# New order tables for the attention stage of a two-layer token kernel

## The chip, the cores and the metric

The kernel runs on one core of one Trainium2 chip. The metric is the device time of one execution in microseconds (us). The engines are TensorE (PE in the profile, PEld for its weight loads), VectorE (DVE), ScalarE (ACT), GpSimd (POOL) and SyncE (SP); each works its own list of instructions in order and waits for the others by semaphores. Three runs of the kernel before took 1610.21, 1616.7 and 1690.98 us.

## The reference, cut to what matters

Sixteen items of 256 tokens, 256 features each, go through two layers. Layer 0 pools an item by masked softmax weights and feeds it to 32 experts. Layer 1 multiplies an item by a matrix that its token picks, and runs a transformer block: attention, then 8 experts. The change lies in layer 1's attention (the cut is mine; 8 batches of 512 in the reference's shape names are 16 items of 256 here):

```python
x = x + L0_ffn(L0_cond(x))                 # 32 experts, top 4
h0 = x @ W[cat_id] + b[cat_id]             # one matrix per item
h = layernorm(h0, ln1_g, ln1_b)
q, k, v = split(h @ Wqkv)                  # 16 heads of 16
q, k = rope(q), rope(k)
scores = where(causal, q @ k.T / sqrt(16), -1e9)
attn = (softmax(scores) @ v) @ Wproj
h1 = h0 + attn
gates = softmax(layernorm(h1, ln2_g, ln2_b) @ Wgate)   # top 2 of 8 experts
x = x + h1 + moe(...)
```

## The kernel before, in words

Four stages follow each other: the pooling, layer 0's experts, the attention stage, and layer 1's experts. In the attention stage an item b is worked in steps, each a few instructions:

- **In front.** POOL gathers the item's rows of layer 0's results with 8 indirect DMAs (`got`, line 1293); DVE adds them, weighted (`combine`, line 1562); PE turns the item (`x_turn`), multiplies it by its matrix (`matrix`, line 1323), DVE normalises (`norm`, `scale`), with POOL working out the inverse deviation (line 1274), and PE turns the result back (`norm_turn`), which ACT copies to hT1.
- **Queries and keys.** For each half of the tokens PE makes queries and keys (`qk`, line 1413), DVE multiplies them by cosines and sines (line 1594), POOL adds and subtracts the products (lines 1302, 1303). PE turns the queries (`turn_qk` 0) and the keys (`turn_qk` 1). The `split` of each takes the high part on ACT (line 1492) and the low part on DVE (line 1598). Then SP's `stack` (line 1269) copies these parts with 8 DMAs of 128 KB for the queries into QS and 8 for the keys into KS. QS and KS are double buffers over items; the parts' tile `parts_qk` is single, as is `rm`, the tile of the rotated products.
- **Attention.** There are 4 groups of heads, and 3 parts of scores in each. PE makes `scores` (lines 1338 to 1347), DVE takes the negated row maximum (`row_max`, line 1554), ACT the exponentials (`exp`, line 1460), PE turns them (`turn_p`, line 1366), ACT copies them (line 1468), PE multiplies by the values (`values`, lines 1379 and 1381) and ACT copies the outcome (line 1474). `v` makes the item's values.
- **Behind.** `outputs` (line 1427) turns the results back and divides them by their sums, `out_turn`, `proj` (line 1323 again), the residual (`base` on POOL, line 1306), the second `norm` and `scale`, `gate_turn` and `gate`. Once for two items the routing follows (`route_shift`, `route_exp`, `route`, `rank`, `place`), and POOL scatters its table with 8 indirect DMAs (`entry`, line 1315).

What sets the order is written out by hand: PE_ROUND, DVE_ROUND, ACT_ROUND, POOL_ROUND and SP_ROUND, one table for each engine. An entry is a step, an offset and further indices. The function `rounds` goes over i from -4 on, and in round i it emits each entry for item i + offset, if there is such an item. So ("scores", -1, 3, 0) in round i is part 0 of group 3 of item i - 1. The engines don't meet at the ends of rounds: a round of one engine may begin well before that of another.

The waits that matter here: the first scores of an item wait until all 16 stack DMAs of that item have landed (line 1333), `stack` 0 waits until the scores of the item two before are done (line 1263), a split waits until the stack of the item before has landed (line 1491), `combine` waits for 4 gathers, and each light step of PE (all but scores, turn_p and values) uses one of two banks in turn and waits until what stood there two light steps before has been copied out (lines 1200 to 1203).

Of the kernel before, what the change touches and what calls it, by code (L numbers as in the profile page):

```python
# [91 lines left out]
def bass_adaln_ffn(nc, io, out):  # L92
    ctx = ExitStack()
    with ctx:
        return _build(nc, ctx, io, out)


def _build(nc, ctx, io, out):
# [6 lines left out]
    def sb(name, shape, dt=F32, scope=ctx):  # L105
        return scope.enter_context(nc.sbuf_tensor(name, shape, dt))
# [5 lines left out]
    normed = nc.dram_tensor("normed", (N + 1, D), F32, kind="Internal").ap()  # L112
# [10 lines left out]
    place = ExitStack()  # L123
# [204 lines left out]
    gate = sb("gate", [P, 2, 512], scope=layer0)  # L328
# [717 lines left out]
    def dve_experts0(e):  # L1046
# [89 lines left out]


    PE_ROUND = (
        ("scores", -1, 0, 1), ("x_turn", 1), ("scores", -1, 0, 2), ("qk", 0, 0), ("scores", -1, 1, 0),
        ("qk", 0, 1), ("scores", -1, 1, 1), ("gate_turn", -3), ("values", -2, 3), ("turn_p", -1, 0, 2),  # L1140
        ("turn_p", -1, 0, 0), ("gate", -3), ("outputs", -2, 0), ("turn_p", -1, 0, 1), ("scores", -1, 1, 2),
        ("turn_qk", 0, 0), ("scores", -1, 2, 0), ("scores", -1, 2, 1), ("outputs", -2, 1), ("turn_p", -1, 1, 2),
        ("values", -1, 0), ("scores", -1, 2, 2), ("out_turn", -2), ("turn_qk", 0, 1), ("turn_p", -1, 1, 0),
        ("turn_p", -1, 1, 1), ("scores", -1, 3, 0), ("proj", -2), ("scores", -1, 3, 1), ("matrix", 1),
        ("turn_p", -1, 2, 2), ("values", -1, 1), ("turn_p", -1, 2, 0), ("scores", -1, 3, 2),
        ("turn_p", -1, 2, 1), ("rank", -3), ("v", 0), ("turn_p", -1, 3, 2), ("values", -1, 2), ("norm_turn", 1),
        ("turn_p", -1, 3, 0), ("turn_p", -1, 3, 1), ("scores", 0, 0, 0))
    DVE_ROUND = (
        ("row_max", -1, 1, 2), ("split", 0, 0), ("outputs", -2, 1), ("row_max", -1, 2, 0), ("route", -3, 1),
        ("row_max", -1, 2, 1), ("row_max", -1, 2, 2), ("route", -3, 2), ("split", 0, 1), ("route", -3, 3),  # L1150
        ("row_max", -1, 3, 0), ("proj", -2), ("row_max", -1, 3, 1), ("matrix", 1), ("norm", 1, 0),
        ("norm", -2, 1), ("row_max", -1, 3, 2), ("scale", 1, 0), ("place", -3), ("combine", 2, 1),
        ("row_max", 0, 0, 0), ("row_max", 0, 0, 1), ("scale", -2, 1), ("row_max", 0, 0, 2), ("qk", 1, 0),
        ("row_max", 0, 1, 0), ("qk", 1, 1), ("row_max", 0, 1, 1), ("combine", 3, 0), ("gate", -2),
        ("route_shift", -2), ("outputs", -1, 0))
    ACT_ROUND = (
        ("exp", -1, 2, 2), ("exp", -1, 3, 0), ("turn_p", -1, 2, 2), ("exp", -1, 3, 1), ("values", -1, 1),
        ("turn_p", -1, 2, 0), ("turn_p", -1, 2, 1), ("exp", -1, 3, 2), ("turn_p", -1, 3, 2), ("v", 0),
        ("norm_turn", 1), ("values", -1, 2), ("turn_p", -1, 3, 0), ("exp", 0, 0, 0), ("x_turn", 2),
        ("exp", 0, 0, 1), ("turn_p", -1, 3, 1), ("exp", 0, 0, 2), ("gate_turn", -2), ("exp", 0, 1, 0),  # L1160
        ("values", -1, 3), ("turn_p", 0, 0, 2), ("exp", 0, 1, 1), ("turn_p", 0, 0, 0), ("turn_p", 0, 0, 1),
        ("split", 1, 0), ("exp", 0, 1, 2), ("route_exp", -2), ("turn_p", 0, 1, 2), ("exp", 0, 2, 0),
        ("out_turn", -1), ("split", 1, 1), ("turn_p", 0, 1, 0), ("exp", 0, 2, 1), ("values", 0, 0),
        ("turn_p", 0, 1, 1))
    POOL_ROUND = (
        ("got", 2, 1, 3), ("norm", 1, 0), ("got", 3, 0, 0), ("norm", -2, 1), ("got", 3, 0, 1), ("entry", -3, 0),
        ("got", 3, 0, 2), ("got", 3, 0, 3), ("qk", 1, 0), ("qk", 1, 1), ("entry", -3, 1), ("entry", -3, 2),
        ("got", 3, 1, 0), ("entry", -3, 3), ("got", 3, 1, 1), ("got", 3, 1, 2), ("base", -1))
    SP_ROUND = (
        ("normed", -2), ("weights", 3), ("stack", 1, 0), ("stack", 1, 1), ("base", -3))  # L1170
    ROUTING = ("route_shift", "route_exp", "route", "rank", "place", "entry")

    def rounds(table):
# [742 lines left out]
```

## Time and profile before

| | us |
|---|---|
| median of 3 runs | 1616.7 |
| the profiled execution, its own time | 1612.6 |
| span of the profile | 1610.8 |
| first scores of item 0 to first scores of item 15 | 494.1 |
| PE busy in those 494.1 us | 421.5 |

The profile is of one execution, told in microseconds from the start of its first instruction. "Idle before" is the time in which an engine stood still ahead of an instruction, with the one that released it behind the arrow; "issue" means that the profile shows no instruction that released it. A busy PE is matrix multiplications in its pipeline, not its peak. The granted clock is 1.00 at 2.4 GHz and 0.50 at 1.2 GHz. A share of DMA over 1 is packets in flight counted on top of each other.

### The profile page before, as it was taken

What the parts mean: (1) busy time and instruction counts of PE and PEld (TensorE: products, weight loads), DVE (VectorE), ACT (ScalarE), POOL (GpSimd) and SP (SyncE); (2) the same over time, 40 slices, a digit from 0 to 9 for tenths busy, and PEclk for the clock granted to TensorE, in tenths of its full rate; (3) what the DMA queues carried; (4) which work ended last, traced back from release to release, by engine and by line L of the source; (5) the groups of instructions that cost most, each with busy time, mean ns of one, the idle gap of its engine ahead of it and who ended that gap; (6) DMA issues with size and microseconds to landing.
All of it is one profiled execution on the core that took longest, in us unless ns stands there. A gap on an engine that the chain in (4) does not pass through costs nothing.

```text
span 1610.8 us, 27526 instructions
## 1 busy us (share of the span) xinstructions
PE 1414.7 (88%) x9776; PEld 1234.1 (77%) x9776; DVE 1026.3 (64%) x2435; ACT 905.2 (56%) x2156; POOL 720.0 (45%) x720
## 2 busy tenths in 40 slices
PE   7987699999999995679998898879826999999996
PEld 5776599999999984456776676656625999999996
DVE  3998477777777756456776776666524655555552
ACT  5886255555555531556776676757724554554452
POOL 0788644434343044333464554633243544554443
PEclk9989899999999997788999998999967999999999
DMA  6421365766666243765677666674543332433212
GB/s 182 138 60 29 87 190 163 191 173 183 181 178 189 78 131 61 109 108 112 125 123 139 122 116 124 116 126 73 73 142 96 93 67 62 97 95 87 50 22 27
DMA packets 139448, 182.00 MB, mean 113 GB/s; under 512 B 22485, under 2 KB 107296, under 8 KB 139312
## 3 DMA queue, kind: packets, MB, share of 16 engines
q1 hardware_dynamic: 111152, 128.28, 32.7%
q0 software_dynamic: 28160, 51.96, 16.2%
q8 instruction: 79, 1.29, 0.4%
q14 instruction: 57, 0.47, 0.1%
HBM read 107.28 MB, written 42.08 MB: 93 GB/s over the span
## 4 chain that ended last, share of the span: by engine, by line
PE 79%; issue 7%; DVE 5%; POOL 3%; DMA 2%; ACT 2%; SPq 1%; POOLq 0%; DVEq 0%; ACTq 0%
PE banks L921 47%; PE banks L1323 5%; PE banks L1366 5%; PE banks L1413 4%; PE banks L440 3%; PE banks L983 2%; PE banks L1379 2%; PE banks L1340 2%; PE banks L1338 1%; PE banks L597 1%; PE banks L1343 1%; PE banks L1347 1%; POOL table L1315 1%; PE banks L1760 1%; PE banks L1427 1%
## 5 line engine op out<-in xcount | busy, mean ns | idle before, releaser
L921 PE MATMUL banks<-hi_x,hi_w 128*128 128x320 f32 (+1 forms) x832 | 286.6, 344 | 10.8 <-DVE hidden L956 5.2
L921 PE MATMUL banks<-lo_x,hi_w 128*128 128x320 f32 (+1 forms) x832 | 285.3, 343 | 0.0
L921 PE MATMUL banks<-hi_x,lo_w 128*128 128x320 f32 (+1 forms) x832 | 285.0, 343 | 0.0
L921 PE MATMUL banks<-hi_w,hi_h 128*128 128x256 f32 x896 | 260.2, 290 | 2.1 <-DVE X L1010 1.7
L921 PE MATMUL banks<-lo_w,hi_h 128*128 128x256 f32 x896 | 253.5, 283 | 0.0
L921 PE MATMUL banks<-hi_w,lo_h 128*128 128x256 f32 x896 | 253.5, 283 | 0.0
L863 POOL DMA_INDIRECT xe<-pooled,idx x160 | 155.3, 971 | 199.9 <-PE banks L983 150.5
L1460 ACT ACTIVATE PN<-banks,smax 128x256 f32<-128x256 f32 (+1 forms) x512 | 181.8, 452 | 107.9 <-DVE smax L1554 107.0
L1747 POOL DMA_INDIRECT out<-X,tab x64 | 106.5, 1664 | 205.0 <-DVE X L1844 190.4
L921 PEld LDWEIGHTS banks<-hi_x,hi_w 128*128 128x128 f32 x832 | 158.0, 190 | 24.2 <-issue 10.6
L921 PEld LDWEIGHTS banks<-hi_w,hi_h 128*128 128x128 f32 x896 | 171.1, 191 | 3.3 <-issue 1.3
L921 PEld LDWEIGHTS banks<-lo_w,hi_h 128*128 128x128 f32 x896 | 171.4, 191 | 0.3
L921 PEld LDWEIGHTS banks<-hi_w,lo_h 128*128 128x128 f32 x896 | 171.2, 191 | 0.0
L1554 DVE TENSOR_REDUCE smax<-banks 128x2 f32<-128x512 f32 (+1 forms) x192 | 128.3, 683 | 63.1 <-PE banks L1340 56.9
L921 PEld LDWEIGHTS banks<-hi_x,lo_w 128*128 128x128 f32 x832 | 157.8, 190 | 13.2
L921 PEld LDWEIGHTS banks<-lo_x,hi_w 128*128 128x128 f32 x832 | 158.1, 190 | 11.8
L1293 POOL DMA_INDIRECT got<-done,slot x128 | 125.5, 981 | 88.9 <-DMA done<-res 56.8
L1805 ACT ACTIVATE hidden<-banks,b1s 128x512 f32<-128x512 f32 x128 | 87.9, 687 | 122.9 <-PE banks L921 122.9
L1833 DVE TENSOR_TENSOR lo_h<-hidden,hi_h 128x512 fp32r<-128x512 f32 x128 | 88.3, 691 | 76.5 <-ACT hi_h L1810 76.5
L956 DVE TENSOR_TENSOR hidden<-gate,banks 128x320 f32<-128x320 f32 (+1 forms) x144 | 73.4, 510 | 84.3 <-PE banks L921 75.0
L1468 ACT ACTIVATE PT<-banks 128x512 f32<-128x512 f32 x192 | 116.5, 624 | 15.1 <-PE banks L1366 14.8
L947 ACT ACTIVATE gate<-banks 128x320 f32<-128x320 f32 (+1 forms) x144 | 65.6, 456 | 98.1 <-PE banks L921 98.0
(186 smaller groups left out, 3082.6 us busy)
## 6 DMA issues: line engine op xcount, KB each, us to landing
w<-in_L_ffn_w SPq DMA_DIRECT2D x96, 256.0 KB, 5.9
done<-res SPq DMA_DIRECT2D x32, 640.0 KB, 3.9
QS<-parts_qk SPq DMA_DIRECT2D x128, 128.0 KB
KS<-parts_qk SPq DMA_DIRECT2D x128, 128.0 KB
BIG<-in_L_ffn_W SPq DMA_DIRECT2D x16, 1024.0 KB, 9.8
mask<-in_c_masks SPq DMA_DIRECT2D x16, 257.0 KB, 2.8
pooled<-XF SPq DMA_DIRECT2D x16, 256.0 KB, 3.2
WS<-in_L_cond_W SPq DMA_DIRECT2D x16, 256.0 KB, 2.7
```

The lines of the kernel that those rows point to most:

```text
L863: e.indirect_dma_start(xe[:, n % NXE, i, :], None, pooled, bass.IndirectOffsetOnAxis(ap=idx0[:, n * NS0 + i:n * NS0 + i + 1], axis=0)).the ...
L921: last = e.matmul(o, a[i], b[j], start=start and k == 0, stop=stop and k == 2, skip_group_check=True)
L956: e.tensor_tensor(hidden[:, i, 0:w], gate[:, i, 0:w], PS[:, up_bank(pt, unit) + 1, 0:w], ALU.mult).then_inc(s_hidden, 1)
L1293: e.indirect_dma_start(got0[:, b % NGA, t, k, :], None, done0, bass.IndirectOffsetOnAxis(ap=slot0[:, TB * b + t, k:k + 1], axis=0)).then_i ...
L1323: last = e.matmul(PS[:, bank, t * D:(t + 1) * D], src[:, c, t * P:(t + 1) * P], w(c), start=(c == 0), stop=(c == DC - 1))
L1366: last = e.transpose(PS[:, bank, k * P:(k + 1) * P], src, ident[:, :])
L1460: e.activation(PN[:, slot, part, x * width:(x + 1) * width], PS[:, part, x * width:(x + 1) * width], ACT.Exp, bias=smax[:, slot, col + x:c ...
L1468: e.activation(PT[:, G % NPN, part, :], PS[:, TBANK + n % 2, :], ACT.Copy).then_inc(s_pt, 1)
L1554: e.tensor_reduce(smax[:, G % NPN, col:col + heads_], PS[:, part, :].rearrange("p (x k) -> p x k", x=heads_), AX.X, ALU.max, negate=True). ...
L1747: e.indirect_dma_start(out_rows, bass.IndirectOffsetOnAxis(ap=who(u, i), axis=0), res1[:, u % 3, i, :], None, bounds_check=N - 1, oob_is_e ...
L1805: e.activation(hidden1[:, m % NHF, :], PS[:, 2 + m % 3, :], ACT.Gelu, bias=b1s[:, n, d:d + 1]).then_inc(s_hidden1, 1)
L1833: e.tensor_tensor(lo_h1[:, d, :], hidden1[:, m % NHF, :], hi_h1[:, d, :].bitcast(F32), ALU.subtract).then_inc(s_h1_lo, 1)
```

## The change

Only the five order tables are different. The steps themselves, what they wait for and what they compute are as before; tiles and buffers are too. In the old tables `qk`, `turn_qk` and `v` of item i stand in round i of PE, in places 4, 6, 16, 24 and 37 of 43, and the first scores of that item stand last in the same round. In the new ones those steps of item i + 1 stand in places 11, 12, 21, 23 and 29 of round i, and the first scores of item i in place 18. Around this `x_turn`, `matrix`, `norm_turn` move up in the same sense, and `values` (3), `outputs`, `out_turn` and `proj` of an item come one round earlier by their offset. On SP the order was normed, weights, the stacks, base, and becomes base, weights, the stacks, normed.

```diff
--- before.py
+++ after.py
@@ -1136,38 +1136,37 @@
 
 
     PE_ROUND = (
-        ("scores", -1, 0, 1), ("x_turn", 1), ("scores", -1, 0, 2), ("qk", 0, 0), ("scores", -1, 1, 0),
-        ("qk", 0, 1), ("scores", -1, 1, 1), ("gate_turn", -3), ("values", -2, 3), ("turn_p", -1, 0, 2),
-        ("turn_p", -1, 0, 0), ("gate", -3), ("outputs", -2, 0), ("turn_p", -1, 0, 1), ("scores", -1, 1, 2),
-        ("turn_qk", 0, 0), ("scores", -1, 2, 0), ("scores", -1, 2, 1), ("outputs", -2, 1), ("turn_p", -1, 1, 2),
-        ("values", -1, 0), ("scores", -1, 2, 2), ("out_turn", -2), ("turn_qk", 0, 1), ("turn_p", -1, 1, 0),
-        ("turn_p", -1, 1, 1), ("scores", -1, 3, 0), ("proj", -2), ("scores", -1, 3, 1), ("matrix", 1),
-        ("turn_p", -1, 2, 2), ("values", -1, 1), ("turn_p", -1, 2, 0), ("scores", -1, 3, 2),
-        ("turn_p", -1, 2, 1), ("rank", -3), ("v", 0), ("turn_p", -1, 3, 2), ("values", -1, 2), ("norm_turn", 1),
-        ("turn_p", -1, 3, 0), ("turn_p", -1, 3, 1), ("scores", 0, 0, 0))
+        ("rank", -3), ("scores", -1, 3, 0), ("turn_p", -1, 2, 2), ("scores", -1, 3, 1), ("values", -1, 1),
+        ("norm_turn", 1), ("turn_p", -1, 2, 0), ("turn_p", -1, 2, 1), ("gate_turn", -2), ("scores", -1, 3, 2),
+        ("qk", 1, 0), ("qk", 1, 1), ("values", -1, 2), ("turn_p", -1, 3, 2), ("gate", -2), ("turn_p", -1, 3, 0),
+        ("turn_p", -1, 3, 1), ("scores", 0, 0, 0), ("scores", 0, 0, 1), ("scores", 0, 0, 2), ("turn_qk", 1, 0),
+        ("values", -1, 3), ("v", 1), ("outputs", -1, 0), ("scores", 0, 1, 0), ("turn_p", 0, 0, 2),
+        ("outputs", -1, 1), ("scores", 0, 1, 1), ("turn_qk", 1, 1), ("scores", 0, 1, 2), ("turn_p", 0, 0, 0),
+        ("out_turn", -1), ("turn_p", 0, 0, 1), ("scores", 0, 2, 0), ("x_turn", 2), ("proj", -1),
+        ("scores", 0, 2, 1), ("matrix", 2), ("turn_p", 0, 1, 2), ("scores", 0, 2, 2), ("turn_p", 0, 1, 0),
+        ("values", 0, 0), ("turn_p", 0, 1, 1))
     DVE_ROUND = (
-        ("row_max", -1, 1, 2), ("split", 0, 0), ("outputs", -2, 1), ("row_max", -1, 2, 0), ("route", -3, 1),
-        ("row_max", -1, 2, 1), ("row_max", -1, 2, 2), ("route", -3, 2), ("split", 0, 1), ("route", -3, 3),
-        ("row_max", -1, 3, 0), ("proj", -2), ("row_max", -1, 3, 1), ("matrix", 1), ("norm", 1, 0),
-        ("norm", -2, 1), ("row_max", -1, 3, 2), ("scale", 1, 0), ("place", -3), ("combine", 2, 1),
-        ("row_max", 0, 0, 0), ("row_max", 0, 0, 1), ("scale", -2, 1), ("row_max", 0, 0, 2), ("qk", 1, 0),
-        ("row_max", 0, 1, 0), ("qk", 1, 1), ("row_max", 0, 1, 1), ("combine", 3, 0), ("gate", -2),
-        ("route_shift", -2), ("outputs", -1, 0))
+        ("route", -3, 3), ("row_max", -1, 2, 0), ("proj", -2), ("row_max", -1, 2, 1), ("norm", -2, 1),
+        ("matrix", 1), ("norm", 1, 0), ("row_max", -1, 2, 2), ("scale", -2, 1), ("scale", 1, 0), ("place", -3),
+        ("combine", 2, 0), ("row_max", -1, 3, 0), ("row_max", -1, 3, 1), ("qk", 1, 0), ("row_max", -1, 3, 2),
+        ("qk", 1, 1), ("combine", 2, 1), ("gate", -2), ("route_shift", -2), ("row_max", 0, 0, 0),
+        ("row_max", 0, 0, 1), ("row_max", 0, 0, 2), ("split", 1, 0), ("route", -2, 1), ("outputs", -1, 0),
+        ("row_max", 0, 1, 0), ("outputs", -1, 1), ("row_max", 0, 1, 1), ("split", 1, 1), ("row_max", 0, 1, 2),
+        ("route", -2, 2))
     ACT_ROUND = (
-        ("exp", -1, 2, 2), ("exp", -1, 3, 0), ("turn_p", -1, 2, 2), ("exp", -1, 3, 1), ("values", -1, 1),
-        ("turn_p", -1, 2, 0), ("turn_p", -1, 2, 1), ("exp", -1, 3, 2), ("turn_p", -1, 3, 2), ("v", 0),
-        ("norm_turn", 1), ("values", -1, 2), ("turn_p", -1, 3, 0), ("exp", 0, 0, 0), ("x_turn", 2),
-        ("exp", 0, 0, 1), ("turn_p", -1, 3, 1), ("exp", 0, 0, 2), ("gate_turn", -2), ("exp", 0, 1, 0),
-        ("values", -1, 3), ("turn_p", 0, 0, 2), ("exp", 0, 1, 1), ("turn_p", 0, 0, 0), ("turn_p", 0, 0, 1),
-        ("split", 1, 0), ("exp", 0, 1, 2), ("route_exp", -2), ("turn_p", 0, 1, 2), ("exp", 0, 2, 0),
-        ("out_turn", -1), ("split", 1, 1), ("turn_p", 0, 1, 0), ("exp", 0, 2, 1), ("values", 0, 0),
-        ("turn_p", 0, 1, 1))
+        ("exp", -1, 3, 0), ("exp", -1, 3, 1), ("exp", -1, 3, 2), ("turn_p", -1, 3, 2), ("values", -1, 2),
+        ("turn_p", -1, 3, 0), ("turn_p", -1, 3, 1), ("route_exp", -2), ("split", 1, 0), ("exp", 0, 0, 0),
+        ("values", -1, 3), ("exp", 0, 0, 1), ("v", 1), ("exp", 0, 0, 2), ("turn_p", 0, 0, 2), ("split", 1, 1),
+        ("exp", 0, 1, 0), ("out_turn", -1), ("x_turn", 2), ("exp", 0, 1, 1), ("turn_p", 0, 0, 0),
+        ("exp", 0, 1, 2), ("turn_p", 0, 0, 1), ("exp", 0, 2, 0), ("turn_p", 0, 1, 2), ("turn_p", 0, 1, 0),
+        ("exp", 0, 2, 1), ("values", 0, 0), ("turn_p", 0, 1, 1), ("exp", 0, 2, 2), ("turn_p", 0, 2, 2),
+        ("values", 0, 1), ("norm_turn", 2), ("turn_p", 0, 2, 0), ("turn_p", 0, 2, 1), ("gate_turn", -1))
     POOL_ROUND = (
-        ("got", 2, 1, 3), ("norm", 1, 0), ("got", 3, 0, 0), ("norm", -2, 1), ("got", 3, 0, 1), ("entry", -3, 0),
-        ("got", 3, 0, 2), ("got", 3, 0, 3), ("qk", 1, 0), ("qk", 1, 1), ("entry", -3, 1), ("entry", -3, 2),
-        ("got", 3, 1, 0), ("entry", -3, 3), ("got", 3, 1, 1), ("got", 3, 1, 2), ("base", -1))
+        ("got", 2, 1, 3), ("entry", -3, 0), ("entry", -3, 1), ("qk", 1, 0), ("qk", 1, 1), ("entry", -3, 2),
+        ("got", 3, 0, 0), ("got", 3, 0, 1), ("got", 3, 0, 2), ("got", 3, 0, 3), ("entry", -3, 3),
+        ("got", 3, 1, 0), ("got", 3, 1, 1), ("base", -2), ("norm", -1, 1), ("got", 3, 1, 2), ("norm", 2, 0))
     SP_ROUND = (
-        ("normed", -2), ("weights", 3), ("stack", 1, 0), ("stack", 1, 1), ("base", -3))
+        ("base", -3), ("weights", 2), ("stack", 1, 0), ("stack", 1, 1), ("normed", -2))
     ROUTING = ("route_shift", "route_exp", "route", "rank", "place", "entry")
 
     def rounds(table):
```

## Rows read from the trace of the kernel before

**Rows 1.** Stage by windows: length, busy time of PE, PEld, DVE, ACT, POOL; PEclk, DMA share, GB/s.

```profile
655.60:1149.70 494.10, 421.49 (x3134) 320.91 (x3134) 330.02 (x809) 336.21 (x893) 226.99 (x249) 0.91 0.66 115
```

**Rows 2.** Waits from 655 to 1165: who for whom, us, times, longest.

```profile
PE banks L1338 <- issue: 69.9, 15, 7.5
DVE X L1562 <- DMA got<-done,slot: 48.9, 12, 7.5
...
PE banks L1338 <- DMA KS<-parts_qk: 12.3, 1, 12.3
```

**Rows 3.** Timeline of PE: start us, us, instruction, count, idle before.

```profile
884.09 0.27 PE L1338 MATMUL banks<-causal,ident_b 128*128 128x256 bf16 x1 [2.89 <-issue]
...
916.25 0.37 PE L1338 MATMUL banks<-causal,ident_b 128*128 128x256 bf16 x1 [5.39 <-issue]
...
924.65 0.66 PE L1379 MATMUL banks<-PT,VP 128*32 128x256 f32 x8
...
926.38 0.96 PE L1442 MATMUL banks<-wgate,h2T 128*128 128x8 f32 x8
927.20 0.64 PE L1427 MATMUL banks<-ident,oT 128*128 128x128 f32 x4
927.67 0.60 PE L1366 MATMUL banks<-ident,PN 128*128 128x128 f32 x4
928.10 0.38 PE L1343 MATMUL banks<-causal,ident_b 128*128 128x512 bf16 x1
...
928.55 0.60 PE L440 MATMUL banks<-ident,rm 128*128 128x128 f32 x4
928.99 0.27 PE L1338 MATMUL banks<-causal,ident_b 128*128 128x256 bf16 x1
...
929.34 0.28 PE L1338 MATMUL banks<-causal,ident_b 128*128 128x256 bf16 x1
...
940.67 1.97 PE L1323 MATMUL banks<-wqkv,hT 128*128 128x256 f32 x8
942.48 0.60 PE L1366 MATMUL banks<-ident,PN 128*128 128x128 f32 x4
...
948.67 0.37 PE L1338 MATMUL banks<-causal,ident_b 128*128 128x256 bf16 x1 [3.32 <-issue]
...
1054.54 0.37 PE L1338 MATMUL banks<-causal,ident_b 128*128 128x256 bf16 x1 [7.52 <-issue]
```

**Rows 4.** Timeline of SP's queue: the stack of one item.

```profile
930.54 5.09 SPq L1269 DMA_DIRECT2D QS<-parts_qk  x8
935.67 6.33 SPq L1269 DMA_DIRECT2D KS<-parts_qk  x8
```

**Rows 5.** Timeline of DVE: the keys' split of two items.

```profile
933.69 0.69 DVE L1598 TENSOR_TENSOR parts_qk<-banks,parts_qk 128x512 fp32r<-128x512 f32 x1 [0.76 <-ACT parts_qk L1492]
...
1036.86 0.67 DVE L1598 TENSOR_TENSOR parts_qk<-banks,parts_qk 128x512 fp32r<-128x512 f32 x1
```

**Rows 6.** Windows: a round's work, after a wait, during a stack; columns as in rows 1.

```profile
884.10:910.80 26.70, 26.70 (x212) 20.78 (x212) 21.73 (x60) 22.26 (x63) 18.64 (x21) 1.00 0.72 114
916.00:919.00 3.00, 2.75 (x10) 2.03 (x11) 2.93 (x7) 0.98 (x3) 0.00 (x0) 0.50 0.26 95
934.00:948.60 14.60, 11.34 (x95) 9.19 (x93) 9.40 (x29) 10.10 (x27) 9.11 (x10) 0.98 1.04 166
```

**Rows 7.** The gathered tile, 655 to 1165: time from DMA to landing.

```profile
DMA to landing us min/median/max: 4.0/7.0/9.7
```

**Rows 8.** Groups on POOL, 655 to 1165: busy us, mean ns, idle before.

```profile
L1293 POOL DMA_INDIRECT got<-done,slot x100 | 97.7, 977 | 24.3 <-issue 22.9
...
L1315 POOL DMA_INDIRECT table<-pair,slot x48 | 47.8, 996 | 17.8 <-issue 13.3 <-DVE slot L312 4.3
...
L1303 POOL TENSOR_TENSOR rm<-rm 128x256 f32<-128x256 f32 x30 | 24.2, 806 | 0.0
...
L1302 POOL TENSOR_TENSOR rm<-rm 128x256 f32<-128x256 f32 x30 | 21.8, 725 | 156.1 <-DVE rm L1594 156.1
```

## The prediction

> **What bounds the kernel now.** I read the waits over the attention stage first, then the stage's windows, then the timelines of PE, SP, DVE and POOL through one round. The waits show one thing that PE stands still for: 15 times it stops ahead of L1338, for 69.9 us together, and once for 12.3 us [rows 2]. L1338 in these places is the first scores of an item, which wait for the stack. The profile names no releaser for the 15 ("issue"), but names the KS DMA for the one before item 0, and in the order table only that step waits there. The timeline agrees: the keys' split of one item starts at 933.69 [rows 5], SP issues the 16 DMAs from 930.54 to 942.00 [rows 4], and the first scores start at 948.67, 15.0 us after that split started [rows 3]. Meanwhile the DMA share is 1.04 at 166 GB/s [rows 6], so the stack lasts as long as its bytes need, and not as long as SP takes to issue them.
>
> From item 0's to item 15's first scores there are 15 rounds in 494.1 us [rows 1], 32.94 us each. The wait is 69.9 / 15 = 4.66 us of each. A round without penalty can be read off too: from 884.09 to 916.25 are 32.16 us with 5.39 us idle [rows 3], which leaves 26.77 us; and from 884.1 to 910.8 PE is busy for all of 26.70 us at a granted clock of 1.00 [rows 6]. The mean round has 32.94 - 4.66 = 28.28 us beside the wait, so 28.28 - 26.77 = 1.51 us of it is what follows a wait: from 916 to 919 the clock is 0.50, the 1.2 GHz level [rows 6]. In the same 26.7 us DVE is busy 21.7, ACT 22.3 and POOL 18.6 us, so PE is the next bound, at some 26.8 us.
>
> **The change, part by part.** *The wait for the stack.* The keys' split must be late enough ahead of the first scores. In the new PE order, what lies between `turn_qk` 1 of item i + 1 and its first scores is a whole round less the stretch from place 18 to place 28. That stretch is four scores of parts 0 and 1, one of part 2, one `turn_qk`, one `values`, `v`, two `outputs` and one `turn_p`. By starts in [rows 3]: scores 0.35 (928.99 to 929.34), part 2 0.45 (928.10 to 928.55), turns 0.43 (927.67 to 928.10), outputs 0.47, `turn_qk` 0.44, `v` 1.81 (940.67 to 942.48), `values` 1.73 - 2 x 0.43 = 0.87 (924.65 to 926.38 holds it and two turns). The sum is 1.40 + 0.45 + 0.44 + 0.87 + 1.81 + 0.94 + 0.43 = 6.3 us. The split starts about 1.2 us after its turn started (copy on ACT, row maximum on DVE ahead of it). In a round of 26.8 us the scores come 26.8 - 6.3 - 1.2 = 19.3 us after the split starts. The two stacks in the rows need 15.0 us and, in the round with the longest wait, 1054.54 - 1036.86 = 17.7 us [rows 3, 5]. Both fit, by 1.6 to 4.3 us. So this wait goes to nothing: -4.66 us a round. If it didn't fit, it would cost what is missing.
>
> *The clock.* Without a wait of several us nothing lowers it: -1.51 us a round, if all new waits are short. The other end is 0 gained. I take all of it, since the stretch in [rows 6] that begins 2.9 us after a halt is at 1.00 throughout; a wait of that size didn't lower it.
>
> *New waits.* The other steps keep their work but have new neighbours. Walking the new PE table with the starts above, each step of a light bank finds what it waits for 0.4 to 0.9 us before its turn: `norm_turn` after `scale`, `qk` after the copy of hT1, `turn_qk` 0 after POOL's two halves of `qk`, `out_turn` after `outputs`. That is a cover of less than 1 us each, and late by x costs x once, not once each. The tightest is POOL in the rounds that scatter a table. There it has 8 gathers and 8 scatters at 0.98 + 0.30 and 1.00 + 0.30 us (20.6 us), the halves of `qk` at 0.73 + 0.81 us twice (3.1 us) [rows 8], and then the base and the two powers; its mean is 227.0 / 15 = 15.1 us a round [rows 1], but in these rounds it comes to some 26 us, as much as PE. The second power (for `scale` of item i + 1) then comes some 1 us later, and `norm_turn` with it. Only every second round has a table, and the gathers end with item 15. I put 0.8 us a round for all new waits; the bounds are 0 and what the old wait was, 4.66 us.
>
> *DVE and ACT* have 21.7 and 22.3 us of work against 26.8 us: they fit, but lose the halt in which they caught up; this is in the 0.8 us.
>
> *The gathers.* All 8 of an item are now issued between the two stacks' start and 3 us after the next round's start, and their landing takes 4.0 to 9.7 us, 7.0 in the middle [rows 7], in a stage with a stack in flight half the time. `combine` 0 comes over 10 us after its last gather, and `combine` 1 some 8 us after. So one that takes 9.7 us holds DVE for 1 to 2 us, which the first scores' distance to their exponentials covers. The 48.9 us that DVE waits for gathers now [rows 2] lie beside the stack's wait; what is left of them shows only if it is over 2 us. Cost 0, and without cover the lateness itself. The Trainium skill says, in "DMA: Bandwidth & Descriptors", section "Issuing engines are not separate DMA queues", that DMAs of SP and POOL run on the same 16 engines and interleave; by that rule moving the gathers under the stack slows both, which is rival 4 below.
>
> *SP.* Its 16 issues take 11.5 us [rows 4] and now stand ahead of `normed`. The buffer of `normed` is double and is wanted again a round and more later; base and weights stand at the front and wait for things done in the round before. Cost 0: SP has 12 us of issues in 27.
>
> *The ends.* The wait for item 0's stack (12.3 us) stays, and item 1's `qk` is now worked inside it. In turn the last round, from item 14's to item 15's first scores, has no `qk`, `turn_qk` and `v` in it: that is at least 1.81 + 0.87 us of PE, and I take 3 us. After item 15's first scores the same work is left as before: 0.
>
> **The sum.** A new round takes 26.8 + 0.8 = 27.6 us, 5.34 less than 32.94; times 15 is 80 us, with 3 us at the end 83 us. The profiled execution's own time was 1612.6 us, so 1530 us. The median of the runs shown is 1616.7 us, 4 us higher, within their spread; I leave 1530.
>
> **The rivals.**
> 1. *Short waits take more.* For it: the covers under 1 us, DVE and ACT at over 80% of a round with each waiting for the other within a group, POOL full in every second round. Against it: in [rows 6] the same chain runs 26.7 us without a halt of PE. At 2 us more a round (29.6): 15 x 3.34 + 3 = 53 us, 1560 us.
> 2. *The clock stays low.* New halts, short but many, might keep it from 1.00 for part of each round. The trace shows low clock only behind the waits for the stack. The price is at most the 1.51 us a round: 1530 + 23 = 1553 us. The Trainium skill has this rule in "TensorE: Matmul & The Clock Gate", section "A second HAM failure mode: psum-queue depth-cycling": frequent micro-idles between groups of matmuls make the clock swing.
> 3. *The stack is still late.* The bytes of a round are the same in less time: the share is 0.66 of 32.94 us [rows 1], 21.7 us, and would be 0.79 of 27.6 us. If the stack then needs 22 us from the split, 3 us of wait come back and with them the clock's 1.5 us: 15 x (5.34 - 4.5) + 3 = 16 us, 1597 us.
> 4. *Slower: the gathers hold DVE.* The four of `combine` 0 are issued while both stacks are. If they land only when the stack drains, up to 6 us after `combine` 0 is due, DVE stands, and behind it the row maxima of group 3, the rotary products of the next item and hence `turn_qk`: PE halts some 6 us and the clock falls. A round is 27.6 + 6 + 1.5 = 35.1 us, 15 x 2.2 - 3 = 30 us over: 1643 us. It decides from some 3.8 us of lateness per round on, where with the clock's 1.5 us the 5.3 us are used up. Against it: no landing took over 9.7 us [rows 7].
> 5. *It does nothing.* If SP's stack could not start earlier, for instance held by the scores of the item before last, all stays at 1613 us. But these scores now stand in place 10 and the first `turn_qk` in place 21, so nothing holds it.
>
> **How the numbers follow.** Forecast 0.66, with a range of its own of 1514 (15 x 6.17 + 6 = 99 us less) to 1550; rival 1 0.15; rival 2 0.04; rival 3 0.06; rival 4 0.05; rival 5 0.04. What a measurement of this kernel can tell from no change is about 2%, 32 us. Faster by over 2% are the forecast, rivals 1 and 2 and a third of rival 3: 0.87. Within 2% are the rest of rival 3, rival 5 and a light rival 4: 0.09. Slower by over 2% is a heavy rival 4 and what no row shows: 0.04. The range of 1514 to 1575 us holds the forecast, rival 2 and most of rival 1; that is 0.66 + 0.04 and most of 0.15, a little over 0.8.
>
> **What would show it.** In the profile after, the wait ahead of L1338 for "issue" is gone or under 10 us in total except before item 0; from item 0's to item 15's first scores it takes 400 to 425 us; the granted clock over it is 0.97 or more; the stack's issues on SP begin some 25 us ahead of the scores that read them. The forecast is wrong if PE waits for DVE or ACT by more than 30 us in the stage (rival 1), if L1562's wait for gathers is followed by one of PE (rival 4), or if L1338 still waits (rival 3).

## The result, and the profile after

The changed kernel takes 1527.5 us in the median of its runs, the kernel before 1617.4 us beside it: a ratio of 0.946, with a 95% interval of 0.9405 to 0.9514. The forecast was 1530 us. The ratios here and below are of fast runs alone, which leaves out one of 1690.98 us of the kernel before, and they differ a little from the quotients of the medians. The profiled execution has a span of 1525.2 us where the old one had 1610.8, so 85.6 us less.

First the attention stage by windows: from item 0's to item 15's first scores, and from 819.80 the length of one round; columns as in rows 1.

```profile
658.06:1062.76 404.70, 394.74 (x3138) 308.22 (x3139) 335.70 (x813) 338.70 (x896) 226.88 (x248) 0.99 0.77 143
819.80:846.50 26.70, 26.70 (x219) 20.96 (x217) 22.55 (x53) 22.26 (x58) 17.33 (x20) 1.00 0.83 154
```

Against [rows 1] the stage has nearly the same work (3138 matmuls for 3134) in 404.7 us instead of 494.1: 89.4 us less. It holds one item's `qk` less (8 matmuls; a `qk` takes 3.59 us at 813.24), which now lies ahead of item 0's scores, and one `gate_turn` and `gate` more. That is some 2 us less for PE, as an estimate from these durations. PE is busy 26.8 us less, and the granted clock is 0.99 where it was 0.91: but for these 2 us, the difference in busy time is the price of the low clock. The other 62.6 us are PE's halts: 10.0 us of the stage are left idle, where there were 72.6. The round in the second row is as PE would have it: busy for all of 26.70 us at 1.00. The same bytes now pass at a share of 0.77.

What PE still waits for by name of a releaser, from 655 to 1080 (who for whom, us in total, times, longest):

```profile
PE banks L1426 <- ACT oT L1473: 3.8, 5, 0.8
PE banks L1337 <- ACT PN L1459: 2.7, 3, 1.4
PE banks L1337 <- DMA KS<-parts_qk: 2.6, 1, 2.6
PE banks L1365 <- ACT PN L1459: 1.6, 2, 1.4
PE banks L440 <- POOL rm L1302: 1.4, 1, 1.4
PE banks L440 <- DVE xn L1528: 1.0, 1, 1.0
```

The 69.9 us in 15 waits of L1338 for "issue" [rows 2] are gone without a rest. The wait for item 0's stack is 2.6 us instead of 12.3. The largest sum now is five waits of up to 0.8 us at `outputs` (L1426). The waits for PN (L1459) lie at the stage's ends, between 664 and 671 and from 1059 on.

The last of them, 1.41 us at 1059.39, is followed by a low clock. Windows of the stage without its ends, and of the time behind that wait:

```profile
661.00:1059.00 398.00, 388.43 (x3109) 302.67 (x3107) 332.50 (x806) 335.98 (x889) 221.86 (x242) 1.00 0.77 143
1061.00:1063.00 2.00, 2.00 (x11) 1.94 (x11) 0.36 (x2) 0.72 (x2) 1.51 (x2) 0.50 0.47 140
```

So what is missing to 1.00 lies at the two ends.

The timeline of PE shows the first scores of item 0, one round (792.11 to 819.79), one wait for rm, and the first scores of item 15 (L1337 is the old L1338):

```profile
658.06 0.37 PE L1337 MATMUL banks<-causal,ident_b 128*128 128x256 bf16 x1 [2.61 <-DMA KS<-parts_qk]
...
792.11 0.27 PE L1337 MATMUL banks<-causal,ident_b 128*128 128x256 bf16 x1
...
797.43 0.63 PE L1426 MATMUL banks<-ident,oT 128*128 128x128 f32 x4 [0.82 <-ACT oT L1473]
...
819.79 0.27 PE L1337 MATMUL banks<-causal,ident_b 128*128 128x256 bf16 x1
...
903.74 0.63 PE L440 MATMUL banks<-ident,rm 128*128 128x128 f32 x4 [1.38 <-POOL rm L1302]
...
1062.76 0.42 PE L1337 MATMUL banks<-causal,ident_b 128*128 128x256 bf16 x1
```

Behind item 0's, first scores carry no wait any more. From one item's to the next it is 26.7 to 26.8 us in the good rounds, 27.23 in the first, 27.6 to 27.7 in four rounds that route, 29.24 in a fifth, and 23.63 in the last. The first 14 rounds have a mean of 27.22 us.

On SP's queue stands the stack that the scores at 819.79 read:

```profile
797.05 5.19 SPq L1268 DMA_DIRECT2D QS<-parts_qk  x8
802.28 5.55 SPq L1268 DMA_DIRECT2D KS<-parts_qk  x8
807.87 0.59 SPq L1244 DMA_DIRECT2D normed<-XN  x1
```

SP begins it 22.7 us ahead of these scores (the forecast had some 25), where in [rows 4, 3] it was 948.67 - 930.54 = 18.1 us. The keys' split of the same item starts at 800.72 on DVE, 19.1 us ahead of them; before, the 15.0 us between split and scores were all that the stack took, and PE stood at its end.

**Where the 85.6 us are.** The stage gives 89.4. Its start comes 2.4 us later (655.65 to 658.06). By the tables item 1's `qk` is now worked ahead of item 0's scores; no run shows that this makes the 2.4 us. From item 15's first scores to the first turn of layer 1's experts it is 70.9 us instead of 69.4, 1.5 us more. The rest is -0.2 us.

### The profile page after: what moved, and what is told of

The parts are those of the page before. It is cut to its first block, busy times and chain, and to the rows that moved or that the text cites. A ratio compares the mean times of both kernels' runs of the same rounds, so it can differ in the third digit from the quotient of the medians.

```text
span 1525.2 us, 27526 instructions
## 1 busy us (share of the span) xinstructions
PE 1392.3 (91%) x9776; PEld 1221.8 (80%) x9776; DVE 1033.8 (68%) x2435; ACT 906.0 (59%) x2156; POOL 721.4 (47%) x720
## 4 chain that ended last, share of the span: by engine, by line
PE 78%; DVE 9%; issue 5%; POOL 3%; DMA 2%; ACT 2%; SPq 1%; POOLq 0%; DVEq 0%; ACTq 0%
PE banks L921 50%; PE banks L1365 5%; PE banks L1322 5%; PE banks L1412 3%; PE banks L440 3%; PE banks L983 2%; PE banks L1378 2%; PE banks L1339 2%; DVE lane_at L504 1%; PE banks L1759 1%; PE banks L1426 1%; DVE X L1561 1%; POOL table L1314 1%; PE banks L1346 1%; PE banks L1337 1%
## 5 line engine op out<-in xcount | busy, mean ns | idle before, releaser
L921 PE MATMUL banks<-hi_x,hi_w 128*128 128x320 f32 (+1 forms) x832 | 286.8, 345 | 10.7 <-DVE hidden L956 5.1
L1459 ACT ACTIVATE PN<-banks,smax 128x256 f32<-128x256 f32 (+1 forms) x512 | 180.3, 443 | 15.9 <-DVE smax L1553 15.9
L1292 POOL DMA_INDIRECT got<-done,slot x128 | 124.5, 973 | 89.4 <-DMA done<-res 56.4
```

What stands on the lines that cost most here:

```text
L921: last = e.matmul(o, a[i], b[j], start=start and k == 0, stop=stop and k == 2, skip_group_check=True)
L1292: e.indirect_dma_start(got0[:, b % NGA, t, k, :], None, done0, bass.IndirectOffsetOnAxis(ap=slot0[:, TB * b + t, k:k + 1], axis=0)).then_i ...
L1459: e.activation(PN[:, slot, part, x * width:(x + 1) * width], PS[:, part, x * width:(x + 1) * width], ACT.Exp, bias=smax[:, slot, col + x:c ...
```

## Experiments: what the stage is made of

The first four kernels ran on another chip: there the kernel before took 1672.4 us in the median of 20 runs. All others ran on one chip where it took 1616.8 or 1617.5 us, as beside the changed kernel above. The four ran again on that chip, and sizes are read from these second runs; "the other chip" below is the one with 1672.4 us.

**The kernel before with half of the keys' bytes.** DMAs and their order on SP are as they were; each of the keys' 8 moves 64 KB instead of 128.

```diff
-                rows_ = slice(s * P // HQ + part * HD, s * P // HQ + (part + 1) * HD)
+                use = HD // 2 if x else HD
+                rows_ = slice(s * P // HQ + part * HD, s * P // HQ + part * HD + use)
...
-                e.dma_start(dst.bitcast(F32), parts_qk[s * P // HQ:(s + 1) * P // HQ, x, high_low, :, :].bitcast(F32)).then_inc(
+                e.dma_start(dst.bitcast(F32), parts_qk[s * P // HQ:s * P // HQ + 4 * use, x, high_low, :, :].bitcast(F32)).then_inc(
```

> The kernel before, in which each of the 8 key DMAs copies half of its rows (64 KB instead of 128; half of the keys' parts stay zero, so the scores are others). As many DMAs, 1.5 MB instead of 2 MB. Theory (the 4.66 us a round that PE waits ahead of the first scores are the bytes of the stack, and 1.51 us more the clock behind it): at the 166 GB/s of the stack's window 0.5 MB are 3.2 us, so the wait falls to some 1.5 us a round and the clock's part goes too: 47 to 70 us less than before, 1545 to 1570 us. Rival (the wait is SP's issuing of 16 DMAs, or the gain lies in the new neighbours of the steps and not in the stack): within 10 us of the kernel before.

> As for the first run of this kernel: if the wait is the bytes of the stack, 47 to 70 us less than the kernel before, where that takes 1617 us; if it is SP's issuing, within 10 us of it.

It took 1577.0 us, a ratio of 0.9736 (0.9685 to 0.9788); on the other chip 0.989 (0.9855 to 0.9925). The wait of first scores, by the waits of this kernel (second run), and its stage by windows:

```profile
PE banks L1339 <- issue: 39.1, 13, 6.2
```

```profile
656.50:1111.50 455.00, 410.75 (x3135) 315.13 (x3135) 329.11 (x809) 335.55 (x893) 227.08 (x248) 0.95 0.55 107
```

16 issues on SP as before, a quarter of the bytes less, and the wait falls from 69.9 us [rows 2] to 39.1. SP's issues don't get shorter: its 8 for the keys take 5.75 us at 829.26 here and 5.06 at 839.39 in the kernel before. So the wait was for bytes to land, not for SP. The gain of 40 us was below the 47 that I had expected at least. The wait itself fell by 30.8 us, 2.1 a round, where 166 GB/s would give 3.2; and the halts that stayed (up to 6.2 us) keep part of the low clock, 0.95. The wait doesn't go by halving one tensor; the order takes it whole.

**The new order with half of the keys' bytes.** The same edit in the changed kernel: if the stack still cost anything there, this would gain.

> The changed kernel with the same halved key DMAs. Theory (in the new order the stack lands before it is needed): no change, within 5 us of 1527 us, and no wait ahead of the first scores. Rival (the new order still pays for the stack, by waits of DVE for gathers or otherwise): 10 us or more less.

> As for the first run of this kernel: the changed kernel with halved key DMAs. If the stack lands in time in the new order, no change: a ratio of 0.945 plus or minus 0.003 to the kernel before, where that takes 1617 us, while the same cut took 40 us off the kernel before (ratio 0.974). If the new order still pays for the stack, 0.935 or less.

1523.7 us, 0.9411 (0.9375 to 0.9446), beside 0.9454 (0.942 to 0.9488) for the changed kernel run again. Rounds are 26.67 to 26.8 us, and 27.6 to 27.7 (once 29.26) where they route, as with all bytes. What 0.5 MB less of the 2 MB of an item bring is 1527.4 - 1523.7 = 3.7 us, and the intervals overlap. In neither kernel do first scores wait, but for item 0's: the stack is hidden.

> The changed kernel itself, once more. In the first four experiments the kernel before took 1672 us and not 1617, and the variants of the changed kernel 1674 and 1677 us, with halts of ACT and DVE of up to 14 us that no instruction in the profile ends. Theory A (those halts belong to the chip, and the change gains where there are none): with the kernel before at 1617 us this takes 1527 us, ratio 0.946; with the kernel before at 1672 us it takes 1660 to 1680 us, ratio 0.99 to 1.005. Theory B (my variants caused the halts): ratio 0.946 in either case.

It gave 1527.4 us, and the stage in windows 404.20 us at 0.99.

**The new order with the stack issued late.** Only SP's table is different; the stack stands last and behind a `normed` that waits for later work.

```diff
-        ("base", -3), ("weights", 2), ("stack", 1, 0), ("stack", 1, 1), ("normed", -2))
+        ("base", -3), ("weights", 2), ("normed", -1), ("stack", 1, 0), ("stack", 1, 1))
```

> The changed kernel with one entry of SP's table moved and advanced: the store of the normed rows of item i - 1 stands ahead of both stacks of item i + 1, so that SP holds the stack until the second scale of item i - 1 is done, about 13 us later than in the changed kernel. All else of the new order stays. Theory: from an item's first scores it takes some 16 us to that scale and then 18 us for the stack, so a round takes 34 to 36 us and the wait of PE ahead of the first scores is back at 7 to 8 us, with the clock at 0.50 behind it: 1635 to 1665 us. Rival (the gain lies in the order on PE, DVE and ACT): 1525 to 1550 us.

> As for the first run of this kernel: 1635 to 1665 us where the kernel before takes 1617 us, if the stack's early place is what gains; 1525 to 1550 us if it is the order on PE, DVE and ACT. The first run already took 1732 us beside 1677 us for a variant with the stack in its early place.

1660.9 us, 1.0266 (1.0232 to 1.0299), slower than the kernel before; on the other chip 1.0364. Its PE timeline and its window:

```profile
909.48 0.37 PE L1337 MATMUL banks<-causal,ident_b 128*128 128x256 bf16 x1 [6.61 <-issue]
...
945.66 0.37 PE L1337 MATMUL banks<-causal,ident_b 128*128 128x256 bf16 x1 [7.98 <-issue]
```

```profile
659.90:1197.50 537.60, 422.07 (x3138) 322.38 (x3138) 336.46 (x810) 342.56 (x905) 229.19 (x249) 0.87 0.59 108
```

All that was won and 44 us more are lost by one queue's order: the halts at first scores are back (111.0 us in 14), with them the clock's fall, to 0.87, and PE's busy time is 422.1 us again, as in [rows 1]. This ties the gain to the stack's early place: the rest of the five new tables, kept here, wins nothing while the stack is late. The other tables are what lets it start early; they were not tried one by one.

**How much room there is.** 8 more DMAs of 128 KB ahead of an item's stack, 1 MB at a time in which the stack itself moved 166 GB/s [rows 6], so some 6.3 us as an estimate. First scores wait for these too (that part of the edit isn't shown).

```diff
+        if x == 0:
+            for j in range(NEXTRA):   # 8
+                e.dma_start(spare[j], parts_qk[0:P // HQ, 0, 0, :, :].bitcast(F32)).then_inc(s_stack[0], 16)
```

> The changed kernel with 8 more DMAs of 128 KB for each item, issued by SP ahead of the queries' stack (they copy the queries' high part to spare rows in memory, and the first scores wait for them too). 1 MB is 6.3 us at 166 GB/s. Theory (the stack has 1.6 to 4.3 us to spare by my sum): a wait of 2 to 4.7 us a round comes back, with up to 1.5 us for the clock: 1555 to 1615 us. Rival (there is far more to spare than I worked out, over 6 us): within 10 us of 1527 us.

> As for the first run of this kernel: 1555 to 1615 us if the stack has 1.6 to 4.3 us to spare, within 10 us of 1527 us if it has over 6 us.

1548.0 us, 0.959 (0.9551 to 0.9629). A round has a mean of 27.96 us (1077.29 - 657.9 over 15), against 26.95 us in the changed kernel's second run: 1.0 us more for 6.3 us of traffic. Its stage by windows:

```profile
657.90:1077.30 419.40, 399.68 (x3139) 309.87 (x3140) 333.59 (x809) 341.06 (x905) 226.33 (x248) 0.98 0.86 175
```

So on average 5.3 us of the 6.3 found room, by that estimate, and the DMA share is 0.86 with the clock at 0.98. The time lies between my two expectations, 1555 us or more and 1537 us or less: I had worked out 1.6 to 4.3 us of spare time, and on average it is more. It isn't the same in every round, for PE halts again ahead of nine of the first scores, 14.1 us in all and up to 3.8.

SP takes about as long to issue the 8 (5.40 us at 827.76) as their bytes would need, so this run doesn't tell which of the two it is that pushes the stack.

**SP's old place for `normed`.**

```diff
-        ("base", -3), ("weights", 2), ("stack", 1, 0), ("stack", 1, 1), ("normed", -2))
+        ("normed", -2), ("weights", 2), ("stack", 1, 0), ("stack", 1, 1), ("base", -3))
```

> The changed kernel with the old order on SP (the store of the normed rows of item i - 2 first, then weights, the stacks, base last). Theory (only what holds the stack back matters, and this store waits for a scale that is done at the start of the round, over 10 us ahead of the stack): within 5 us of the changed kernel. Rival (the new order on SP is a needed part of the gain): over 15 us longer.

1529.0 us, 0.9449 (0.9408 to 0.9491): nothing, the rounds are the same but for one of 28.09 us where the changed kernel has 27.67. Of SP's two orders tried, the one counts in which a `normed` that isn't ready stands ahead of the stack, as above; where it is ready in time, its place doesn't matter.

## Experiments: the short waits that are left

The good round is 26.7 to 26.8 us, the mean 27.2. The trace of the changed kernel shows in which rounds the difference lies, and the chain behind it. From the timeline of a round that routes, all engines:

```profile
789.53 0.75 POOL L1301 TENSOR_TENSOR rm<-rm 128x256 f32<-128x256 f32 x1
...
790.22 0.74 POOL L1302 TENSOR_TENSOR rm<-rm 128x256 f32<-128x256 f32 x1
...
790.48 3.75 DVE L1561 SCALAR_TENSOR_TENSOR X<-got,w_pick,X 128x256 f32<-128x256 f32 x4
...
790.89 0.75 POOL L1301 TENSOR_TENSOR rm<-rm 128x256 f32<-128x256 f32 x1
...
791.58 0.73 POOL L1302 TENSOR_TENSOR rm<-rm 128x256 f32<-128x256 f32 x1
...
794.35 0.19 DVE L187 TENSOR_REDUCE nm<-lgs 128x4 f32<-128x32 f32 x1
...
794.57 0.30 ACT L195 ACTIVATE ex<-lgs,nm 128x8 f32<-128x8 f32 x1 [1.61 <-issue]
...
796.91 0.37 ACT L1473 ACTIVATE oT<-banks 128x256 f32<-128x256 f32 x1
...
797.43 0.63 PE L1426 MATMUL banks<-ident,oT 128*128 128x128 f32 x4 [0.82 <-ACT oT L1473]
```

Read it backwards. PE's `outputs` waits 0.82 us for ACT's copy of oT. ACT had stood 1.61 us ahead of the first exponential of `route_exp` (L195), for the maximum that DVE makes at 794.35: it ends at 794.54, though the profile names no releaser. And DVE is late since its second `combine`, four instructions from 790.48, took 3.75 us, where the first takes 2.04. The rotation of POOL runs beside it.

**A shorter rotation on POOL.** It rotates a quarter of the columns; the second of its two instructions is cut in the same way.

```diff
-                e.tensor_tensor(half[:, 0, :, 0, :], half[:, 0, :, 0, :], half[:, 1, :, 1, :], ALU.subtract)
+                e.tensor_tensor(half[:, 0, 0:2, 0, :], half[:, 0, 0:2, 0, :], half[:, 1, 0:2, 1, :], ALU.subtract)
...
```

> The changed kernel, in which POOL rotates only a quarter of the columns of queries and keys (the rest stays as DVE left it, so the scores are others). In the changed kernel the second combine of DVE takes 3.7 us for 4 operations, the first 2.0 us, and POOL's rotations run beside the second. Theory (they slow each other): that combine falls to 2.0 to 2.6 us, and the 0.8 us that PE waits for ACT's copy of the values in the rounds with routing goes. Rival (the gathers and the stack in flight slow it): it stays at 3.7 us.

1525.3 us in its one run. In the stage all `combine` but two take 2.03 to 2.05 us now (those two 2.09 and 2.38), and three of the four rounds of 27.6 to 27.7 us take 26.67. The groups' row of `combine`, this kernel's first and the changed kernel's behind it (busy us, mean ns of one):

```profile
L1561 DVE SCALAR_TENSOR_TENSOR X<-got,w_pick,X 128x256 f32<-128x256 f32 x128 | 62.1, 486 | 5.6 <-DMA got<-done,slot 2.2
```

```profile
L1561 DVE SCALAR_TENSOR_TENSOR X<-got,w_pick,X 128x256 f32<-128x256 f32 x128 | 76.6, 599 | 5.0 <-DMA got<-done,slot 1.4
```

The chain is as read: with the rotation short, DVE's instructions are fast, and the round of 29.24 us takes 27.61. The time hardly moved for all that: four rounds by 1 us and one by 1.6 would be 5.6 us, but one of those four took 31.0 us, 4.3 over 26.7. In it ACT halts 3.27 us ahead of the copy of oT, which no instruction of the profile explains, and PE behind it 2.49 us; from 796.60 to 800.00 the clock is 0.51. The cut also shortens POOL's own work; the two effects are not apart in this run.

**`route_exp` behind `values`.** ACT's `route_exp` stands three places later, so that the copy of oT doesn't wait behind it, and DVE's first step of `route` one place later. The rows are cut to what moves.

```diff
 ACT_ROUND
-        ("route_exp", -2), ("split", 1, 0), ("exp", 0, 0, 0), ("values", -1, 3),
+        ("split", 1, 0), ("exp", 0, 0, 0), ("values", -1, 3), ("route_exp", -2),
 DVE_ROUND
-        ("route", -2, 1), ("outputs", -1, 0),
+        ("outputs", -1, 0), ("route", -2, 1),
```

> The changed kernel with two swaps: on ACT the exponentials of the routing stand behind the copy of the values instead of ahead of the queries' split, and on DVE the first routing step behind the first outputs. Theory (in the 7 rounds with routing PE waits 0.8 us for ACT's copy of the values, because ACT waited there for the routing's maximum on DVE): these waits go, rounds of 27.65 us become 26.8 us, 5 us less in all, a ratio of 0.942. Rival (POOL's scatters fill those rounds, as my prediction had it): the rounds stay at 27.65 us, no change.

1531.1 us, 0.9455 (0.9425 to 0.9485): no gain. Its waits say why:

```profile
PE banks L1365 <- ACT PN L1459: 5.2, 8, 1.4
PE banks L1426 <- DVE parts_qk L1597: 1.7, 4, 0.6
PE banks L1426 <- ACT oT L1473: 1.3, 2, 0.7
```

These are over the whole execution, in which the changed kernel has 3.0 us in 3, none, and 4.4 us in 6 for the same three. The wait for oT went down to 1.3 us, but L1365 waits 2.2 us more for the exponentials, and 1.7 us for DVE came. The rounds that route take 27.6 to 28.4 us. PE's wait has moved from one copy of ACT to others and to DVE; this order alone doesn't take it away.

## The chip on which nothing was won

On the other chip two variants of the changed kernel gained nothing against the kernel before: with half of the keys 1674.1 us, 1.0019 (0.9993 to 1.0045), with the 8 DMAs 1676.9 us, 1.0037 (1.0004 to 1.007). The changed kernel itself did not run there. With half of the keys' bytes, the stage takes 497.2 us there in the new order (708.61 to 1205.79) and 477.9 in the old (704.56 to 1182.43); where the kernel before takes 1617 us, it is 403.4 and 455.0. So on the other chip the new order loses 94 us in the stage and the old one 23. The waits of the new order with half of the keys, from 600 to 1300, and the longest of them in ACT's timeline:

```profile
DVE rsum L1604 <- remote: 46.3, 8, 9.3
...
ACT VP L1499 <- remote: 39.5, 12, 6.2
PE banks L1427 <- issue: 38.5, 12, 6.0
ACT oT L1474 <- remote: 18.6, 3, 13.6
PE banks L1427 <- ACT oT L1474: 15.9, 3, 14.6
```

```profile
886.73 0.38 ACT L1474 ACTIVATE oT<-banks 128x256 f32<-128x256 f32 x1 [13.60 <-remote]
```

ACT and DVE stand for up to 13.6 us, with no instruction of the profile as releaser ("remote"), ACT in this stage nearly always right behind an `exp` (L1460); PE stands behind them, 14.56 us in the longest case. In its second run, where the kernel before takes 1617.5 us, the same program has no wait with this releaser, and takes 150 us less. All four kernels have such halts on the other chip, the old order with half of the keys too (DVE 40.5 us in 12 at L1555), so the new order doesn't make them. Nor is that chip alone in having them: three kernels have one elsewhere, ahead of the copy of oT, of 0.3, 0.5 and 3.27 us, the last in the round of 31.0 us above. What holds ACT and DVE stays open: no run told it apart. It bounds the result: the 5.4% were measured where the kernel before takes 1617 us.

## Why the prediction was right

- **The stack's wait** was to go whole, 4.66 us a round. It did: 69.9 us in 15 waits before, none after, but for item 0's. Half of the keys in the old order shows that it was for bytes, and the stack issued late in the new one that its place is what counts. The time between the keys' split and the scores was worked out at 19.3 us and is 19.1. The room was put at 1.6 to 4.3 us; by the estimate above it is 5.3 on average, and less in the nine rounds that halted.
- **The clock's** 1.51 us a round came back. PE's busy time in the stage fell from 421.5 to 394.7 us, 26.8 us in all or 1.8 a round; without the 2 us of work that left the stage it is some 1.65. "Without a wait of several us nothing lowers it" was too strong: behind the 1.41 us at 1059.39 PE runs at 0.50. It does so behind the same wait in the changed kernel's second run, but not in the kernel with SP's old place for `normed` (1.42 us at 1060.58). Behind the 1.38 us at 903.74 the clock stays at 1.00, and so it did in the kernel before behind the 2.89 us at 884.09, where the stretch of [rows 6] starts (directly behind that wait, and not 2.9 us after it).
- **New waits** were put at 0.8 us a round and are 27.22 - 26.8 = 0.42. Here the size was off, and the mechanism was mostly another. I had blamed POOL, full in rounds that scatter a table: it shows once, in the round of 29.24 us, with PE's 1.38 us for rm at 903.74 in it, and there DVE's `combine` is slowed as well (3.62 us at 899.41). In the four rounds of 27.6 to 27.7 us it is the `combine` that POOL slows, then DVE's maximum, then ACT. I had priced `combine` by its rows alone, without what runs beside it.
- **The gathers** were put at 0. From 655 to 1165 they land after 5.1 to 10.6 us, 7.2 in the middle, where [rows 7] has 4.0, 7.0, 9.7; counted from 640 on, the longest took 11.0 us after and 10.7 before. The Trainium skill's rule that DMAs of SP and POOL interleave ("DMA: Bandwidth & Descriptors", section "Issuing engines are not separate DMA queues") would have them slower beside a stack: the 0.2 us in the middle go that way, and no run ties them to it. It cost nothing, since DVE's wait for them fell from 48.9 us [rows 2] to 1.4. By the tables `combine` 0 now stands in the round after its four gathers, where it stood in the same round.
- **The clock under many short waits** (rival 2): with eleven waits of 0.2 to 1.4 us behind the one for item 0 the granted clock is 1.00 from 661 to 1059, and 0.50 for a few us behind the last of them, so the stage has 0.99. The swings of the Trainium skill's rule ("TensorE: Matmul & The Clock Gate", section "A second HAM failure mode: psum-queue depth-cycling"), which the prediction had weighed, didn't show here but for that one.
- **SP's order** at 0: shown, 1529.0 us with the old place of `normed`.
- **The ends** were to give 3 us: the last round is 3.6 us shorter than the mean of the others. The size came out, the reason did not: `turn_qk` and `v` of item 15 are in that round (1040.31, 1041.65 and 1045.48), and what it lacks is a `qk`, of 3.59 us. That its size is near the 3 us is luck. But the start is 2.4 us later, and the tail 1.5 us longer, where I had written 0 for both. In the tail `base` of POOL (L1305, 1.28 us at 1106.96) stands between the scatters of the last table; that it makes the 1.5 us was not tried.

By terms: the sum was 83 us and the span fell by 85.6. The first 14 rounds gave (32.91 - 27.22) x 14 = 80, the last 33.38 - 23.63 = 9.8, and the start and the tail took 3.9. The forecast had 0.4 us a round too much for waits (6 us) and nothing for what start and tail took (4 us): two errors of opposite sign, so it was nearer than its terms.

## What to carry to other kernels

In this kernel the wait that no instruction released, ahead of work that reads a copied tile, was explained by the time from the last write of that tile, so measure that first: if the distance is what the bytes take, start the copy a half round earlier rather than make it smaller. A halt of several us was paid twice here, in the halt and mostly in the clock behind it, so take it whole: cutting the wait from 69.9 to 39.1 us gave 1616.8 - 1577.0 = 40 us, taking it away 1616.8 - 1527.4 = 89. When a step is moved under another engine's work, cost it with what now runs beside it.

## What the runs showed of the hardware

DVE's `combine` reads two tiles of SBUF (the memory beside the engines) at 128x256, and POOL's rotation reads SBUF too. Without a rotation beside them, four of DVE's instructions take 2.04 us. With two of POOL's beside them (818.31 and 819.18 in the changed kernel) they take 2.73, and POOL's go from 0.73 to 0.90 us. With two and the end of a third beside them (from 790.48, in the rows above) they take 3.75, and POOL's stay at 0.75 and 0.73; here the first of DVE's four, which started while POOL's was running, takes 2.13 us alone, where one has 0.48 otherwise. With the rotation at a quarter (0.33 us each) DVE keeps 2.04 us nearly everywhere and POOL's two beside it take 0.49 and 0.56; with four of POOL's in a row beside it (899.25) it takes 2.38. So 0.69 us are lost for two of POOL's instructions in one case and 1.71 us in the other, and hardly any with short ones. The Trainium skill has such a rule in "SBUF — State Buffer", section "Who interferes with whom": a DVE instruction with two SBUF inputs and a GpSimd instruction that reads SBUF contend for a shared read interface, its port pair is an exclusive lock, and the order of issue decides who blocks. 0.69 us are about one of POOL's instructions and 1.71 us somewhat over two, and who loses is now the one and now the other, which agrees. The prediction priced `combine` without this rule.
